# A gated cross-attention and feed-forward layer: joint weighing of a pair's tiles on GpSimd, short scalings moved from VectorE to ScalarE, and a new order of the steps and the drain

## The reference

```python
x = x + tanh(g_xattn) * xattn(layernorm(x), ctx, seg)      # x: 4 x 1024 x 256, ctx: 4 x 77 x 256 -> indices below 128
x = x + tanh(g_ffn) * ffn(layernorm(x))

# xattn: 16 heads of 16; token i looks at entries seg[i], seg[i]-1, seg[i]-2, seg[i]-3 of its batch
qh = heads(q @ Wq.T);  k, v = split(kv_src @ Wkv.T)
k_sel, v_sel = kh[gather], vh[gather]                      # 4 entries a token, index clipped, < 0 masked
probs = softmax((qh . k_sel) / 4)                          # over the 4 entries
out = (sum of probs * v_sel) @ Wo.T

# ffn: weights rounded to 8 bits (scale by column of W_in, by row of W_out), activations to 16 bits (one scale)
hidden = gelu(quant16(x) @ quant8(W_in) + b_in)            # 256 -> 1024, exact gelu
out = quant16(hidden) @ quant8(W_out) + b_out              # 1024 -> 256
```

## Time and profile before

| | us |
|---|---|
| median of 3 runs | 311.67 |
| lowest, highest | 310.97, 313.34 |
| the profiled execution | 311.57 |
| its span | 309.4 |
| attention loop (25.9 to 160.5) | 134.6 |
| drain (160.5 to 183.5) | 23.0 |
| expand (183.5 to 239.3) | 55.8 |
| largest hidden value (239.3 to 247.0) | 7.7 |
| contract (247.0 to 303.0) | 56.0 |
| busy PE, DVE, ACT, POOL | 281.3, 276.0, 252.2, 165.7 |

### The profile page before, as it was taken

The page is one execution under the profiler, slowest core; times in us unless marked ns, Lnnn a source line. Parts: engine busy times, 40 slices in busy tenths (PEclk is TensorE's granted clock), DMA queues, the critical chain, the costliest instruction groups (busy, mean ns, idle before and its releaser), DMA issues.

```text
span 309.4 us, 6195 instructions
## 1 busy us (share of the span) xinstructions
PE 281.3 (91%) x1946; PEld 214.1 (69%) x1946; DVE 276.0 (89%) x523; ACT 252.2 (82%) x514; POOL 165.7 (54%) x144
## 2 busy tenths in 40 slices
PE   6999999999997898998985669999999899999991
PEld 5776787887876787887783534444444688888881
DVE  0899999999999999999989883999998799999991
ACT  2789899899897896788761867999999699999980
POOL 1136899989998799999998203233335001111110
PEclk9999999999999999999999989999999999999997
DMA  7993210000000000000000001013111004444446
GB/s 208 335 407 122 65 51 22 0 2 2 0 3 0 1 2 0 2 0 3 1 1 2 0 0 68 3 78 126 68 68 68 2 0 67 72 68 68 68 68 138
DMA packets 7606, 17.46 MB, mean 56 GB/s; under 512 B 1414, under 2 KB 3918, under 8 KB 7198
## 3 DMA queue, kind: packets, MB, share of 16 engines
q1 hardware_dynamic: 5167, 12.80, 11.3%
q0 software_dynamic: 1008, 3.67, 7.8%
q10 hardware_dynamic: 1407, 0.69, 0.8%
HBM read 7.82 MB, written 7.86 MB: 51 GB/s over the span
## 4 chain that ended last, share of the span: by engine, by line
PE 49%; POOL 21%; DVE 18%; issue 5%; ACT 3%; DMA 2%; ACTq 0%; DVEq 0%; POOLq 0%
PE bank L1043 18%; PE bank L1010 18%; POOL vsel L357 10%; POOL vsel L360 7%; DVE prod L1116 4%; PE bank L830 4%; PE bank L810 3%; DVE bank L1122 3%; POOL o L364 3%; PE bank L788 2%; DMA bin_ld<-in_L_ffn_b_in_dram 2%; POOL rstd L348 1%; POOL both_rstd L345 1%; DVE xres L1172 1%; ACT xn L481 1%
## 5 line engine op out<-in xcount | busy, mean ns | idle before, releaser
L810 PE MATMUL bank<-kvtab,onehot 80*128 80x256 f16 x512 | 64.9, 273 | 5.9 <-ACT vsel L496 3.3
L357 POOL TENSOR_TENSOR vsel<-vsel,pr 128x1024 f32<-128x1024 f32 x31 | 59.9, 1933 | 8.6 <-DVE pr L1152 8.6
L810 PEld LDWEIGHTS bank<-kvtab,onehot 80*128 80x128 bf16 x512 | 48.6, 97 | 18.8 <-ACT vsel L496 5.2
L690 ACT ACTIVATE hidden<-bank,bin__58,zscale 128x512 f32 x64 | 47.8, 789 | 3.8
L1010 PE MATMUL bank<-xhi,win 128*128 128x512 f16 x128 | 49.4, 386 | 1.2 <-ACT win L410 1.2
L1010 PE MATMUL bank<-xlo,win 128*128 128x512 f16 x128 | 49.3, 385 | 0.0
L1478 DVE SCALAR_TENSOR_TENSOR hlo<-hq,rel_wout,hhi 128x512 f16<-128x512 int16 x64 | 45.6, 742 | 0.0
L1422 DVE TENSOR_REDUCE hmax<-hidden (+1 forms) x31 | 36.3, 1213 | 7.4 <-ACT hidden L690 7.0
L360 POOL TENSOR_TENSOR vsel<-vsel 128x512 f32<-128x512 f32 x31 | 39.4, 1273 | 2.4
L389 POOL TENSOR_TENSOR xres<-xres,bout 128x1024 f32<-128x1024 f32 x8 | 18.8, 2358 | 38.8 <-DVE xlo L1417 38.8
L1116 DVE TENSOR_TENSOR prod<-bank,q 128x1024 f32<-128x1024 f32 x32 | 38.8, 1213 | 0.8 <-PE bank L810 0.8
(11 more groups left out here) (165 smaller groups left out, 499.8 us busy)
## 6 DMA issues: line engine op xcount, KB each, us to landing
out_dram<-xres SPq DMA_DIRECT2D x7, 512.0 KB, 2.6
out_dram<-y POOLq DMA_DIRECT2D x7, 512.0 KB, 5.4
xres<-in_x_dram SPq DMA_DIRECT2D x3, 1024.0 KB, 16.5
onehot<-onehot SPq DMA_DIRECT2D x9, 160.0 KB, 2.6
xres<-in_x_dram SPq DMA_DIRECT2D x2, 512.0 KB, 7.0
win_ld<-in_L_ffn_W_in_dram SPq DMA_DIRECT2D x1, 1024.0 KB, 12.8
wout_ld<-in_L_ffn_W_out_dram SPq DMA_DIRECT2D x1, 1024.0 KB, 20.7
wkv_ld<-in_L_xattn_Wkv_dram SPq DMA_DIRECT2D x1, 512.0 KB, 5.2
```

The source lines that it names most:

```text
L357: pool.tensor_tensor(v3, v3, pr[k][:, t].rearrange("p o h -> p (o h)").unsqueeze(2).broadcast_to([P, KW * H, HD]), ALU.mult).then_inc(s_pv, 1)
L690: act.activation(hidden[:, g, f, :], bank, ACT.Gelu, bias=bin_[:, f:f + 1], scale=zscale[:, f:f + 1]).then_inc(s_h, 1)
L810: mm = pe.matmul(dst[:, off * D:(off + 1) * D], onehot[0:U, off, bass.ds(tile * P, P)], kvtab[:, b, part, col:col + D], start=(part == 0), ...
```

## The change

GpSimd's `weigh_v`, called for each tile, becomes `weigh_pair`, called once a step, with the same three operations over both tiles. `vsel` becomes two buffers of a pair; a v copy waits for the pair before last. The floors of the weight maxima are no longer a VectorE scalar operation: the maxima go into column 0 of `peak_win` and `peak_wout`, whose column 1 holds the floor, and a reduction over the two makes the floored value. The scalings of `sc_win`, `sc_wout`, `diag`, `rel_wout` and `bout` go to ScalarE. `weigh_last` writes its product contiguously and reduces with a stride. The rest is order.

```diff
-        vsel = [a_r.put(f"vsel{i}", [P, KW, D], F32) for i in range(4)]
+        vsel = [a_r.put(f"vsel{i}", [P, 2, KW, D], F32) for i in range(2)]
+            pool.memset(peak_win[:], AMAX_FLOOR).then_inc(s_const, 1)
+            pool.memset(peak_wout[:], AMAX_FLOOR).then_inc(s_const, 1)
...
+            def weigh_pair(u, k):
+                nt = 2 if u < NP - 1 else 1
+                v = vsel[k][:, 0:nt]
+                pool.wait_ge(s_vc2, 2 * u + nt)
+                pool.wait_ge(s_p, u + 1)
+                v3 = v.rearrange("p t o (h d) -> p (t o h) d", h=H)
+                pool.tensor_tensor(v3, v3, pr[k][:, 0:nt].rearrange("p t o h -> p (t o h)").unsqueeze(2)
+                                   .broadcast_to([P, nt * KW * H, HD]), ALU.mult).then_inc(s_pv, 1)
+                pool.wait_ge(s_pv, u + 1)
+                pool.tensor_tensor(v[:, :, 0:2, :], v[:, :, 0:2, :], v[:, :, 2:4, :], ALU.add).then_inc(s_pv2, 1)
+                pool.wait_ge(s_pv2, u + 1)
                 if first(u, 2):
                     pool.wait_ge(s_oTp, u - 1)
+                pool.tensor_tensor(o[k][:, 0:nt, :], v[:, :, 0, :], v[:, :, 1, :], ALU.add).then_inc(s_o, 1)
...
 # ScalarE
             def round_win(hf):
+                act.wait_ge(s_wilev, hf + 1)
+                v = slice(hf * FC // 2, (hf + 1) * FC // 2)
+                act.activation(sc_win[:, v], sc_win[:, v], ACT.Copy, scale=W_LEVELS).then_inc(s_winsc, 1)
+            def wout_scales():
+                act.wait_ge(s_wlev, 2)
+                act.wait_ge(s_ident, 2)
+                act.activation(sc_wout[:], sc_wout[:], ACT.Copy, scale=W_LEVELS).then_inc(s_woutsc, 1)
+                act.activation(diag[:], ident[:], ACT.Copy, scale=top_wout[:, 0:1]).then_inc(s_wrow, 1)
+            def wout_ratio():
+                act.wait_ge(s_wtop, 1)
+                act.activation(rel_wout[:], amax_wout[:], ACT.Copy, scale=top_wout[:, 2:3]).then_inc(s_rel, 1)
...
             def copy_v(u, t):
                 n = 2 * u + t
                 act.wait_ge(s_vp, n + 1)
-                if first(n, 4):
-                    act.wait_ge(s_o, n - 3)
+                if first(u, 2):
+                    act.wait_ge(s_o, u - 1)
...
 # ScalarE's step: kv_high before squares1; sums2 before evac_xn2T; copy_v(i-1, 0) before the second sums1;
 # the second squares1 behind norm2, rounding and copy_v(i-1, 1); var_eps last
-            ROUND_AT = {10: 0, 11: 1, 12: 2, 13: 3, 14: 4, 15: 5}
-            FIRST1 = {2: 1, 3: 3, 4: 4, 5: 6, 6: 7, 7: 8, 9: 9, 10: 11, 11: 12}
-            SECOND1 = {2: 2, 4: 5, 9: 10}
+            ROUND_AT = {9: 0, 10: 1, 12: 2, 13: 3, 15: 4, 16: 5}
+            FIRST1 = {2: 1, 3: 3, 4: 4, 5: 6, 6: 7, 7: 8, 9: 9, 10: 10, 11: 11}
+            SECOND1 = {2: 2, 4: 5, 11: 12}
 # ScalarE's drain
+            var_eps(NP - 3, 1)
             norm2(NP - 4, 0)
-            var_eps(NP - 3, 1)
             round_win(0)
             evac_oT(NP - 1, 1, ps_q)
+            evac_xn2T(NP - 4, 0)
             norm2(NP - 3, 1)
             var_eps(NP - 2, 0)
-            evac_xn2T(NP - 4, 0)
             half_win(0)
+            round_win(1)
             norm2(NP - 2, 0)
-            var_eps(NP - 1, 1)
             evac_xn2T(NP - 3, 1)
             norm2(NP - 1, 1)
+            half_win(1)
+            act.wait_ge(s_tanh, 1)
+            act.activation(bout[:], bout[:], ACT.Copy, scale=tanhs[:, 1:2]).then_inc(s_bias, 1)
             evac_xn2T(NP - 2, 0)
-            round_win(1)
-            half_win(1)
             keep_win8(0)
+            evac_xn2T(NP - 1, 1)
             keep_win8(1)
-            evac_xn2T(NP - 1, 1)
+            wout_ratio()
...
 # TensorE's drain: the first win_T behind the 30 idle transposes; win_T(1) before attn_out(NP - 2)
             transpose_o(NP - 2, 0, (s_p, NP), ps_w)
-            attn_out(NP - 2, 0)
-            transpose_xn2(NP - 4, 0, (s_xn2T, NP - 4))
             pe.wait_ge(s_lastpv, 1)
             win_T(1)
-            pe.wait_ge(s_rel, 1)
+            attn_out(NP - 2, 0)
+            pe.wait_ge(s_wtop, 1)
             transpose_o(NP - 1, 1, (s_q, NP), ps_q)
+            idle_work(ps_w, 8)
+            transpose_xn2(NP - 4, 0, (s_xn2T, NP - 4))
+            idle_work(ps_w, 8)
             attn_out(NP - 1, 1)
-            transpose_xn2(NP - 3, 1, (s_xn2T, NP - 3))
+            idle_work(ps_w, 8)
             win_back(0)
+            transpose_xn2(NP - 3, 1, (s_xn2T, NP - 3))
+            idle_work(bank01[:, 0:512], 6)
             transpose_xn2(NP - 2, 0, (s_xn2T, NP - 2))
...
 # VectorE
-                dve.scalar_tensor_tensor(out=pw.rearrange("p (h d o) -> p o h d", h=H, o=KW),
-                                         in0=ps_v[:].rearrange("p (o h d) -> p o h d", o=KW, h=H), scalar=kvs[:, 1, NB - 1:NB],
+                dve.scalar_tensor_tensor(out=prod[1][:].rearrange("p o (h d) -> p (o h) d", h=H),
+                                         in0=ps_v[:].rearrange("p (n d) -> p n d", d=HD), scalar=kvs[:, 1, NB - 1:NB],
...
 # VectorE's step: stats2 behind the first qk_sum; wout_levels and aggregate behind the second qk; wout_amax last
-            WOUT_AT = (7, 8)
+            WOUT_AT = (6, 7)
             def wout_levels():
-                dve.wait_ge(s_ident, 2)
-                link(dve.tensor_scalar(amax_wout[:], amax_wout[:], AMAX_FLOOR, None, ALU.max))
-                link(dve.tensor_reduce(top_wout[:, 0:1], amax_wout[:], AX.X, ALU.max))
-                dve.tensor_scalar(diag[:], ident[:], top_wout[:, 0:1], None, ALU.mult).then_inc(s_wrow, 1)
-                link(dve.reciprocal(sc_wout[:], amax_wout[:]))
-                dve.tensor_scalar(sc_wout[:], sc_wout[:], W_LEVELS, None, ALU.mult).then_inc(s_woutsc, 1)
+                link(dve.tensor_reduce(amax_wout[:], peak_wout[:], AX.X, ALU.max))
+                dve.tensor_reduce(top_wout[:, 0:1], amax_wout[:], AX.X, ALU.max).then_inc(s_wlev, 1)
+                dve.reciprocal(sc_wout[:], amax_wout[:]).then_inc(s_wlev, 1)
...
 # VectorE's drain, whole
+            softmax_end(NP - 1, 1)
             residual(NP - 3, 1)
-            softmax_end(NP - 1, 1)
+            weigh_last(NP - 1, 1)
             stats2(NP - 3, 1)
-            weigh_last(NP - 1, 1)
+            norm_bias(NP - 4, 0)
+            aggregate(NP - 3, 1)
             win_amax(0)
             win_levels(0)
-            norm_bias(NP - 4, 0)
-            aggregate(NP - 3, 1)
-            wout_ratio()
+            wout_top()
             residual(NP - 2, 0)
-            largest(NP - 4, 0)
             stats2(NP - 2, 0)
+            aggregate(NP - 2, 0)
             norm_bias(NP - 3, 1)
-            aggregate(NP - 2, 0)
             win_amax(1)
             win_levels(1)
+            largest(NP - 4, 0)
             residual(NP - 1, 1)
             norm_bias(NP - 2, 0)
             stats2(NP - 1, 1)
             aggregate(NP - 1, 1)
+            dve.wait_ge(s_mv, dve_pairs(NP - 1) + 1)
+            dve.tensor_scalar(ve[1][:], mv[1][:, :, 1], LN_EPS, None, ALU.add).then_inc(s_ve, 1)
             largest(NP - 3, 1)
+            norm_bias(NP - 1, 1)
             largest(NP - 2, 0)
-            norm_bias(NP - 1, 1)
             norm2_half()
-            dve.tensor_scalar(bout[:], bout[:], tanhs[:, 1:2], None, ALU.mult).then_inc(s_bias, 1)
```

More of the change, by code:

```diff
@@ L1193, in step @@
                     softmax_end(i - 2, k)
-                if on(4) and i > 4 and not on_act(i - 4):
-                    stats2(i - 4, k)
                 if i in FIRST_AT:
@@ L1203, in step @@
                         aggregate(0, 0)
[L1204 to L1205 removed]
                 if on(1):
                     qk_sum(i - 1, 1 - k, 0)
+                if on(4) and i > 4 and not on_act(i - 4):
+                    stats2(i - 4, k)
                 if i in KV_AT:
                     kv_low(KV_AT[i])
[L1210 to L1213 removed]
                 if on(5):
```

101 lines of the change are left out of this document (49 added, 52 removed).

## The result

The changed kernel took 303.25 us (median; 302.65 to 303.38), the kernel before 312.5 (310.97 to 313.6) in the same comparison. The ratio is 0.9704, 95% interval 0.9653 to 0.9754: faster by 3.0%. Forecast were 306.0 us and a range of 303.2 to 309.8. Direction and range held, but the median lies only 0.05 us above the range's low end. The difference is 9.2 us in this comparison, and 8.4 from the 311.67 that the forecast counted from, where 5.6 were forecast. The profiled execution has a span of 300.8 us instead of 309.4.

A forecast was written before the change was run, and what follows sets the result against it. VectorE was taken to bound the loop at 8.82 us a step, TensorE 0.4 behind, GpSimd following. Loop -3.1 (-2.85 - 0.57 + 0.3) and drain -2.5 from 311.6 gave 306.0 us; range 303.2 to 309.8.

The forecast's parts named there:

- Rival D: Loop: GpSimd, not VectorE, was the bound; 0.7 us more for each of 11 steps, 301 or so; chance 0.04.
- a follower with a small backlog: Loop: GpSimd runs as full as VectorE but starts a weighing 1.3 us after its probabilities are ready.
- The scalings: Loop, `wout_levels` on VectorE: 3.4 us removed, 0.55 left, gain 2.85 us, all on the bound engine.
- The wait for `rstd` in the last step: Last loop step: VectorE's 0.57 us wait for GpSimd goes with the joint weighing.
- `stats2` and `aggregate` only change places: VectorE's loop order: the two only swap positions, counted at no gain.
- ScalarE's delay: Loop step 11: a second layer-1 statistics piece makes ScalarE late; priced 0 to 0.8 us, taken 0.3.
- Rival B: GpSimd: joint instructions save nothing, the backlog and the 0.57 stay; 307.9 us; chance 0.10.
- Rival C: Loop: ScalarE's v copy held by the joint buffer, 0.8 us a step, next residual late; 315.6 us; chance 0.09.
- A wait of this kind: Sign against the prediction: wrong if ScalarE's v copy waits for GpSimd's o.
- Rival A: Drain: ScalarE, with its work in one fixed order, becomes the bound and gives the gain back; 308.5 us; chance 0.13.
- the step that priced the strided product: Drain, VectorE: product with contiguous output takes 1.25 us instead of 2.07, bounds 1.2 and 2.07.
- The clock: First feed-forward matmuls at granted clock 0.50: counted at nothing; if the clock held, 1.25 us more would go.

The follow-up runs named there:

- e1: Kernel before with nothing but the joint weighing (`weigh_pair`, two-buffer `vsel`, their waits): 315.07 us, ratio 1.010.
- e2: Kernel before with only the scalings moved to ScalarE and floors made by reductions; order and weighing by tile as before: 306.76 us, ratio 0.985.
- e12: Changed kernel with `stats2` and `aggregate` back in VectorE's old places in the loop: 303.49 us, ratio 0.973 to the kernel before.
- e3: Kernel before with only VectorE's loop order changed (`stats2` behind the first `qk_sum`, `aggregate` between second product and its sum): 312.91 us, ratio 1.002.
- e4: Changed kernel with the old weighing by tile (four single `vsel` buffers, `weigh_v`): 305.55 us, ratio 0.983 to the kernel before.
- e7: Changed kernel without the idle transposes (fillers) it added to the drain: 302.16 us, ratio 0.970 to the kernel before.
- e9: Changed kernel with VectorE's maximum `largest` put between the softmax's maximum and `shift`: 303.47 us, ratio 0.972 to the kernel before.
- e10: As e9, plus the two halves of `stats2` between the softmax's sum, reciprocal and probabilities: 302.65 us, ratio 0.968 to the kernel before.
- e6: Changed kernel with an unused VectorE maximum over 128x64 added in each of four loop steps: 304.08 us, ratio 0.976 to the kernel before.
- e8: Changed kernel with the last tile's strided sum made by two VectorE additions: 302.87 us, ratio 0.974 to the kernel before.
- e11: e10 without the idle transposes (fillers) that the change added to the drain: 302.62 us, ratio 0.969 to the kernel before.

## Why the prediction was right, and what it missed

**The bound.** The forecast took VectorE for the loop's bound although the chain named GpSimd, and that held: e1, which shortens only GpSimd, won nothing in an ordinary step, and e2, which shortens only VectorE, won 3.0 us of loop. Rival D (GpSimd was the bound) is out for the kernel before. But it was closer than I had it: from 129.87 to the next pair's first product GpSimd takes 8.78 us, against 8.82.

```profile
138.65 1.94 POOL L357 TENSOR_TENSOR vsel<-vsel,pr 128x1024 f32<-128x1024 f32 x1
```

I had read "a follower with a small backlog" and not what follows from it, that the bound passes over after 0.04 us of gain. Rival D also had a wrong sum: 0.7 for 11 steps is 7.7 us and not 5, so that only TensorE's 8.45 a step held its time near 302.

**Loop, forecast -3.1, measured -5.2.** The scalings were sized at -2.85; e2 gives -3.0, as the levels take 0.39 us instead of 0.55. The wait for `rstd` in the last step (-0.57) went, and so did one of 0.2 two steps earlier. The loop went past its own bound of -3.4. The step that failed is "`stats2` and `aggregate` only change places", which was put at nothing: `aggregate` went between a product and its sum, 0.12 us in each step that has it, and the steps are 8.70 and not 8.82. e12 shows it with 0.8 us of loop, and e3 in its steps, though not in its sum. ScalarE's delay (+0.3) did not come: no step from 9 to 13 is longer than 8.74. These make -4.6. The last 0.6 lies in steps 6 to 9, into which `wout_amax` and the levels were moved (0.35, the levels now between a product and its sum), and in the last three; no experiment separates it, and none isolates ScalarE's new order.

**The parts are not a sum.** Alone, three parts give +2.8 (e1), -3.0 (e2) and -0.8 (e3) in the loop, which adds up to -1.0, not to -5.2. The forecast said that a lock could now be held for nearly 4 us and counted nothing, because no such scaling was left; right for the whole change, and e1 puts a number on what it would have cost otherwise. It missed the other coupling, that the joint weighing frees what the new order gains: without it (e4) the loop loses 3.0 of the 5.2.

**GpSimd's joint instructions** took 3.69, 2.36 and 1.28, forecast 3.67, 2.36 and 1.27, and the idle time before the product appeared, released by `pr`. Rival B is out: a pair with its inverse root takes 8.15 us (99.49 to 107.64) against 8.81 (129.87 to 138.68). The Trainium skill, Perfetto Trace Analysis, section "GPSIMD Engine Instruction", says that the reported durations don't compose and that start-to-start spacing should be used. It does not say that joining saves nothing, as I had made it say for rival B. Here both measures agree to 0.08 us (the product of 3.69 is followed after 3.76), and the durations of three sizes foretold the next one to 0.02 us.

**Rival C,** ScalarE held by the joint buffer, is there at its place, but 0.5 us in two waits instead of 0.8 a step. A wait of this kind was named as a sign that the prediction is wrong; it came, and was too short to matter.

**Drain, forecast -2.5, measured -2.8 (bounds 0 and -3.1).** Rival A is out. Two terms inside were off and met each other. Wrong was the step that priced the strided product: 1.28 for 1.25 forecast, yet product and sum together are 3.26 now and 3.29 before, since the stride only moved to the reader. I had costed one instruction of the pair. Against it, the waits on GpSimd were worth 1.3 (e2), the joint weighing of pair 14 0.8 (after against e4), and the new order 0.7 (e4 against e2), which is what is left of it after the 0.6 that the fillers cost (e7).

**The clock.** Counted at nothing, with a bound of -1.25. It was 1.00 at the first matmuls, and expand is 0.5 us shorter (0.8 in e2); the rest of the 1.25, as I read it, is covered by VectorE's rounding, since the first matmuls now wait for `xhi` (0.34 us at 177.48). In other executions it fell in the drain, as in e9, whose drain has the changed kernel's code and is 1.5 us longer:

```profile
160.00:165.00 5.00, 2.91 (x14) 2.40 (x13) 4.83 (x16) 3.13 (x9) 2.90 (x4) 0.85 0.01 3
165.00:170.00 5.00, 5.00 (x32) 4.74 (x31) 2.70 (x9) 3.25 (x8) 0.70 (x1) 0.81 0.00 0
```

e10, with the same drain code, has 1.00 in both windows and 20.9 us. One profile a kernel can't tell whether code or chance decides this, and 1 to 2 us of every drain in the table above hang on it. The mean granted clocks of all runs tell more. Chance has a part: three runs of e9 have 0.991 and took 303.80 to 305.29 us, the other three have 0.997 to 0.999 and took 301.65 to 303.15. The code has one too. Of the kernel before, 28 of 33 runs lie at 0.995 or below. With the new fillers (the changed kernel, e4, e6, e8, e9, e10, e12) 5 of 32 do, without them (e7, e11) 10 of 12. e10 and e11, which differ in the fillers alone, have 1 and 6 of 6. So the fillers probably do hold the clock, and what that wins is about what they cost in TensorE's way (302.65 against 302.62). They are not all of it: e2, with the old drain, has 1 of 4. In the kernel before, the five runs above 0.995 have a median of 310.5 us and the others 312.1, so that 1 to 2 us of the 9.2 go with the clock, which the forecast counted at nothing.

**The range.** That it held is luck in part. Its low end without rival D was 303.8, above the 303.25 measured, and D, for which it was lowered to 303.2, did not happen.

## What to carry to other kernels

When two engines are full, compare their steps by start-to-start distance: the gap between them is the whole worth of an edit on the longer one, until the other is shortened as well; test parts together and not only one by one. Look for VectorE instructions far longer than their shape, and whether they end with a GpSimd instruction: then change their kind (a reduction) or their engine (ScalarE), and do it before making GpSimd's instructions longer. When a stride is moved from a writer to a reader, price both.
